# Layer 1 of seven of eight experts as Strassen products, in an fp32 mixture-of-experts kernel with two task towers

## What is computed

```python
B, D, E, T = 512, 1024, 8, 2; H1, H2, DO = 1024, 512, 256; TH1, TH2 = 512, 256
h = relu(einsum('bi,eio->beo', x, eW1) + eb1)          # layer 1: 8 experts, 1024 x 1024
h = relu(einsum('beh,eho->beo', h, eW2) + eb2)         # layer 2: 1024 x 512
expert_out = einsum('beh,eho->beo', h, eW3) + eb3      # layer 3: 512 x 256
gates = softmax(einsum('bi,tie->bte', x, gW) + gb)
tin = einsum('bte,bed->btd', gates, expert_out)
th = relu(einsum('btd,tdh->bth', tin, tW1) + tb1)
th = relu(einsum('bth,tho->bto', th, tW2) + tb2)
out = sigmoid(einsum('bth,tho->bto', th, tW3) + tb3)
```

## Time and profile before

| | us |
|---|---|
| median of 3 runs | 606.9 (606.57 to 607.07) |
| the profiled execution | 606.77 |
| its span in the profile | 605.0 |
| PE busy | 600.1 (2,629 matmuls) |
| DVE busy | 281.4 |
| ACT busy | 191.7 |
| POOL busy | 39.0 |

### The profile page before, as it was taken

One profiled execution on the slowest core, in us unless ns is written; L12 is line 12 of the kernel. 1 busy time (PEld: TensorE's weight loads), 2 busy tenths in 40 slices (PEclk: granted clock), 3 DMA queues, 4 the chain that ended last, 5 costly groups with the idle time before them and its releaser, 6 DMA issues.

```text
span 605.0 us, 7134 instructions
## 1 busy us (share of the span) xinstructions
PE 600.1 (99%) x2629; PEld 491.6 (81%) x2629; DVE 281.4 (47%) x391; ACT 191.7 (32%) x227; POOL 39.0 (6%) x37
## 2 busy tenths in 40 slices
PE   9999999999999999999999999999999999999998
PEld 5888888888888888888888888888888888888775
DVE  7634346346245343364443562453433634435592
ACT  3422325214233233223332242332332233322543
POOL 1000000030000200030000300003000300003000
PEclk9999999999999999999999999999999999999999
DMA  8930098205331073302522053310733025220000
GB/s 312 324 104 1 3 357 280 94 0 204 108 104 35 0 243 104 104 0 96 181 94 79 0 189 123 104 35 0 243 104 104 0 81 196 92 81 0 1 1 0
DMA packets 33435, 63.25 MB, mean 105 GB/s; under 512 B 1921, under 2 KB 7169, under 8 KB 33298
## 3 DMA queue, kind: packets, MB, share of 16 engines
q1 hardware_dynamic: 33106, 58.64, 29.5%
q0 software_dynamic: 176, 4.23, 1.8%
q10 hardware_dynamic: 144, 0.26, 0.1%
HBM read 63.08 MB, written 0.04 MB: 104 GB/s over the span
## 4 chain that ended last, share of the span: by engine, by line
PE 97%; DMA 1%; DVE 1%; ACT 1%; SPq 0%; issue 0%; ACTq 0%
PE bank L199 32%; PE bank L201 32%; PE bank L200 32%; DMA w_raw<-eW 1%; DVE w_lo L535 0%; ACT w_hi L440 0%; PE bank L354 0%; PE bank L353 0%; PE bank L424 0%; SPq L221 0%; DVE gated L713 0%; DVE h_lo L548 0%; ACT task_in L527 0%; ACT gated L523 0%; PE bank L371 0%
## 5 line engine op out<-in xcount | busy, mean ns | idle before, releaser
L535 DVE TENSOR_TENSOR w_lo<-w_raw,w_hi 128x1024 fp32r<-128x1024 f32 x99 | 121.0, 1224 | 239.2 <-ACT w_hi L440 238.9
L199 PE MATMUL bank<-x_hi,w_hi 128*128 128x512 f32 x524 | 204.1, 389 | 0.5 <-issue 0.4
L201 PE MATMUL bank<-x_hi,w_lo 128*128 128x512 f32 x524 | 203.9, 389 | 0.0
L200 PE MATMUL bank<-x_lo,w_hi 128*128 128x512 f32 x524 | 203.8, 389 | 0.0
L440 ACT ACTIVATE w_hi<-w_raw 128x1024 fp32r<-128x1024 f32 x99 | 104.8, 1059 | 282.7 <-PE bank L201 262.8
L199 PE MATMUL bank<-h_hi,w_hi 128*128 128x512 f32 x336 | 131.1, 390 | 0.1
L200 PE MATMUL bank<-h_lo,w_hi 128*128 128x512 f32 x336 | 130.8, 389 | 0.0
L201 PE MATMUL bank<-h_hi,w_lo 128*128 128x512 f32 x336 | 130.7, 389 | 0.0
L199 PEld LDWEIGHTS bank<-x_hi,w_hi 128*128 128x128 f32 x524 | 98.3, 188 | 21.8 <-issue 0.8
L201 PEld LDWEIGHTS bank<-x_hi,w_lo 128*128 128x128 f32 x524 | 98.4, 188 | 20.5
L200 PEld LDWEIGHTS bank<-x_lo,w_hi 128*128 128x128 f32 x524 | 98.4, 188 | 20.4
(11 more groups left out here) (61 smaller groups left out, 74.8 us busy)
## 6 DMA issues: line engine op xcount, KB each, us to landing
w_raw<-eW SPq DMA_DIRECT2D x103, 512.0 KB, 4.1
gates_all<-gates_dram POOLq DMA_DIRECT2D x1, 4096.0 KB, 14.3
w_raw<-tW SPq DMA_DIRECT2D x4, 512.0 KB, 3.4
gates_all<-xT SPq DMA_DIRECT2D x7, 256.0 KB, 6.5
w_raw<-eW SPq DMA_DIRECT2D x2, 256.0 KB, 4.3
gates_all<-xT ACTq DMA_DIRECT2D x1, 256.0 KB, 3.4
prm<-small SPq DMA_DIRECT2D x1, 164.0 KB, 8.0
gates_dram<-turned POOLq DMA_DIRECT2D x1, 32.0 KB, 2.0
```

The lines of the kernel that those rows point to most:

```text
L199: pe.matmul(bank[:], weights_hi, moving_hi, start=first, stop=False)
L200: pe.matmul(bank[:], weights_hi, moving_lo, start=False, stop=False)
L201: return pe.matmul(bank[:], weights_lo, moving_hi, start=False, stop=last)
L535: dve.tensor_tensor(w_lo[:, j % RING, :], raw_piece(j), w_hi[:, j % RING, :].bitcast(F32), ALU.subtract).then_inc(w_ready, 1)
```

## The change

Layer 1 of expert 0 stays as it was. For experts 1 to 7 the product W1ᵀx is cut into 2x2 blocks: the inner dimension into two halves of four k tiles, the output into m tiles i and i+4 (a pair, four of them), the batch into halves of 256 columns. Each pair is seven block products in place of eight (Strassen's scheme in Winograd's form, with 15 sums), each of 4 k tiles by 3 matmuls of 256 columns: 84 matmuls to a pair, 336 to an expert.

- Four sums are of x alone. They are made once, in expert 0 (`sum_x`, `t_cast`, `split_t`), into `t_hi` and `t_lo`.
- Four are of weights: DVE adds blocks of 128x512 (`sum31` makes two at once, `sum2`, `sum4`). Three weight blocks are used as they are. So each pair has 7 blocks of 128x512 to split: ACT and DVE do 3 + 2 + 2 of them (`plain`, `sums31`, `sums24`; in pair 2 the last two singly).
- Seven sums are of results. Each product has half a bank of its own. ACT takes one of them with both signs (`p1_take`), DVE makes the sums in five operations (`combine_base` and `_united` two each, `_lower` one, `_cross` two, the last three of 256 columns), and ACT and DVE split a pair's two hidden tiles (`pair_h1`, `pair_h1_lo`). DVE does the sums of pair i-1 between the weight sums of pair i+1.
- The ring has 10 slots of 128x512, the raw buffer four units of 128x1024; W1 of a pair is one transfer of 128x2048 (1 MB) from an array laid out for it on the host. W3 takes two slots of the same ring.
- Elsewhere: the high part of a hidden tile is now written by ACT straight from the bank (a second ACT operation, in place of DVE's cast), and DVE forms relu and difference in one operation; layer 2 takes its k tiles in the order 0, 4, 1, 5 ...; the gates of one expert are loaded at a time by POOL; `gated` has two buffers, so DVE's third gate product waits for POOL's first add. Layers 2 and 3 and the towers have the matmuls that they had.

```diff
+SLOT = 512
+RING = 10
+UNIT = 2 * SLOT
+UNITS = 4
...
+PAIRS = H1 // P // 2
+KK = KX // 2
...
+PRODUCTS = [(1, 0, "x", 1, 0),
+            (0, 0, "x", 0, 0),
+            (3, 0, "t", 1, 0),
+            (2, 1, "t", 0, 1),
+            (2, 0, "t", 0, 0),
+            (1, 1, "t", 1, 1),
+            (3, 1, "x", 1, 1)]
+NP = len(PRODUCTS)
...
-BANK_HIDDEN1 = [4, 5, 6, 7, 0, 1, 2, 3]
-BANK_HIDDEN2 = [6, 7, 0, 1]
-BANK_OUT3 = [4, 5]
...
+BANK_HIDDEN1 = [0, 1, 2, 3, 4, 5, 6, 7]
+BANK_HIDDEN2 = [4, 5, 6, 7]
+BANK_OUT3 = [0, 1]
...
+def used(e, u):
+    return USED0 + (e - 1) * USED + u + 1
+def free(e, u):
+    if u < NP:
+        return USED0 + (e - 1) * USED - 6 + u
+    return USED0 + (e - 1) * USED + u - RING + 1
...
+        X_SUMS = [((0, 1), (0, 0), (0, 0)),
+                  ((0, 1), (1, 1), (0, 1)),
+                  ((1, 1), (0, 0), (1, 1)),
+                  ((1, 0), (1, 1), (1, 0))]
...
+            def pair(e, i):
+                ready = splits(e) + 3 * i
+                for n, (bank, nh, source, kh, xh) in enumerate(PRODUCTS):
+                    if n == 0:
+                        if i == 0:
+                            pe.wait_ge(gated_ready, 1 + GATED * (e - 1))
+                        elif i == 1:
+                            pe.wait_ge(h2_staged, K3 * e)
+                        else:
+                            pe.wait_ge(combined, PAIRS * (e - 1) + i - 1)
+                        pe.wait_ge(slot_ready, ready + 1)
+                    if n == 3:
+                        pe.wait_ge(slot_ready, ready + 2)
+                    if n == 5:
+                        pe.wait_ge(slot_ready, ready + 3)
+                    slot = (NP * i + n) % RING
+                    to = banks[4 * (i % 2) + bank][:, nh * HALF:(nh + 1) * HALF]
+                    hi, lo = (x_hi, x_lo) if source == "x" else (t_hi, t_lo)
+                    for kk in range(KK):
+                        cols = slice(kk * P, (kk + 1) * P)
+                        mm = triple(pe, to, w_hi[:, slot, cols], w_lo[:, slot, cols],
+                                    block_of(hi, kh, xh)[:, kk, :], block_of(lo, kh, xh)[:, kk, :],
+                                    kk == 0, kk == KK - 1)
+                    mm.then_inc(slot_used, 1)
...
+            def plain_hi(e, i):
+                u = 2 * (i % 2)
+                if u == 0:
+                    act.wait_ge(landed[0], (3 + 4 * (e - 1) + i // 2 + 1) * DMA)
+                else:
+                    act.wait_ge(landed[2], (3 + 3 * (e - 1) + i // 2 + 1) * DMA)
+                pair_free(e, i, NP * i + 2)
+                act.activation(wide(pair_slots(i, 0, 3)), w_raw[:, u * UNIT:u * UNIT + 3 * SLOT], ACT.Copy) \
+                    .then_inc(slot_hi, 1)
...
+            def take_hidden2(done, m):
+                act.wait_ge(l2_done, K3 * (done - 1) + m + 1)
+                bank, bias = banks[BANK_HIDDEN2[m]], prm_of("b2", done * K3 - K3 + m)
+                if m < 2:
+                    act.wait_ge(h1_ready, K2 + PAIRS * (done - 1))
+                else:
+                    act.wait_ge(h2_ready, K3 * (done - 1) + m - 1)
+                act.activation(h2_hi[:, m, :], bank[:], ACT.Relu, bias=bias)
+                act.activation(stage[:, m % 2, :], bank[:], ACT.Identity, bias=bias).then_inc(h2_staged, 1)
...
+            def sum31(e, i):
+                landed_pair(e, i)
+                dve.wait_ge(slot_ready, splits(e) + 3 * i if i > 0 else splits(e - 1) + 3 * PAIRS)
+                dve.tensor_tensor(sums[:, 0:2, :], raw_blocks(i, 1, 2),
+                                  raw_blocks(i, 3, 1).broadcast_to([P, 2, SLOT]), ALU.add).then_inc(summed, 1)
+            def sum2(e, i):
+                dve.wait_ge(summed, 3 * PAIRS * (e - 1) + 3 * i + 1)
+                dve.tensor_tensor(sums[:, 2, :], sums[:, 1, :], raw_blocks(i, 1, 1)[:, 0, :],
+                                  ALU.add).then_inc(summed, 1)
+            def sum4(e, i):
+                dve.wait_ge(summed, 3 * PAIRS * (e - 1) + 3 * i + 2)
+                dve.tensor_tensor(sums[:, 3, :], sums[:, 2, :], raw_blocks(i, 0, 1)[:, 0, :],
+                                  ALU.add).then_inc(summed, 1)
...
+            def combine_base(e, i):
+                dve.wait_ge(p1_staged, PAIRS * (e - 1) + i + 1)
+                dve.wait_ge(slot_used, used(e, NP * i + 5))
+                if i == 0:
+                    dve.wait_ge(h2_ready, K3 * e)
+                else:
+                    dve.wait_ge(h1_ready, K2 + PAIRS * (e - 1) + i)
+                dve.tensor_tensor(quarter[:, 0:5:4, :], bank_of(i, 1), p1[:], ALU.add).then_inc(based, 1)
+            def combine_united(e, i):
+                dve.wait_ge(based, PAIRS * (e - 1) + i + 1)
+                dve.tensor_tensor(quarter[:, 1:3, :], bank_of(i, 2), quarter[:, 4:5, :].broadcast_to([P, 2, HALF]),
+                                  ALU.add).then_inc(united, 1)
+            def combine_lower(e, i):
+                dve.wait_ge(united, PAIRS * (e - 1) + i + 1)
+                dve.scalar_tensor_tensor(quarter[:, 3, :], bank_of(i, 2)[:, 0, :], prm_of("b1", e * K2 + MG + i),
+                                         quarter[:, 2, :], ALU.add, ALU.add).then_inc(lowered, 1)
+            def combine_cross(e, i):
+                dve.wait_ge(slot_used, used(e, NP * i + 6))
+                dve.scalar_tensor_tensor(quarter[:, 1, :], bank_of(i, 3)[:, 1, :], prm_of("b1", e * K2 + i),
+                                         quarter[:, 1, :], ALU.add, ALU.subtract)
+                dve.wait_ge(lowered, PAIRS * (e - 1) + i + 1)
+                dve.scalar_tensor_tensor(quarter[:, 2, :], bank_of(i, 3)[:, 0, :], prm_of("b1", e * K2 + MG + i),
+                                         quarter[:, 2, :], ALU.add, ALU.add).then_inc(combined, 1)
...
             with dve.Fori(1, E) as e:
-                expert(e)
+                sum31(e, 0)
+                sum2(e, 0)
+                sum4(e, 0)
+                plain_lo(e, 0)
+                sums31_lo(e, 0)
+                for m in range(K3 - 1):
+                    hidden2_lo(e, m)
+                sums24_lo(e, 0)
+                hidden2_lo(e, K3 - 1)
+                for i in range(PAIRS - 1):
+                    if i > 0:
+                        combine_base(e, i - 1)
+                    sum31(e, i + 1)
+                    if i > 0:
+                        combine_united(e, i - 1)
+                    sum2(e, i + 1)
+                    if i > 0:
+                        combine_lower(e, i - 1)
+                        combine_cross(e, i - 1)
+                    sum4(e, i + 1)
+                    plain_lo(e, i + 1)
+                    if i > 0:
+                        pair_h1_lo(e, i - 1)
+                    sums31_lo(e, i + 1)
+                    sums24_lo(e, i + 1)
+                combine_base(e, PAIRS - 2)
+                combine_united(e, PAIRS - 2)
+                combine_lower(e, PAIRS - 2)
+                combine_cross(e, PAIRS - 2)
+                pair_h1_lo(e, PAIRS - 2)
+                w3_lo(e)
+                for i in range(3):
+                    w2_lo(e, i)
+                combine_base(e, PAIRS - 1)
+                combine_united(e, PAIRS - 1)
+                combine_lower(e, PAIRS - 1)
+                combine_cross(e, PAIRS - 1)
+                pair_h1_lo(e, PAIRS - 1)
+                w2_lo(e, 3)
                 gate_expert(e)
...
+                        dve.wait_ge(added, GATED * (done - 1) + n + 1)
```

More of the change, by code:

```diff
@@ L197, in triple @@
         def triple(pe, bank, weights_hi, weights_lo, moving_hi, moving_lo, first, last):
[L199 to L201 removed]
+            pe.matmul(bank, weights_hi, moving_hi, start=first, stop=False)
+            pe.matmul(bank, weights_hi, moving_lo, start=False, stop=False)
+            return pe.matmul(bank, weights_lo, moving_hi, start=False, stop=last)
@@ new lines, in layer2 @@
+            def layer2(e, between=None):
+                first = isinstance(e, int)
+                order = by_tile(range(0, 6), MG) + by_bank(range(6, 8), MG)
+                for i, (n, m) in enumerate(order):
+                    k = ORDER2[n]
+                    if m == 0:
+                        if n % 2 == 0:
+                            pe.wait_ge(slot_ready, (KX + n // 2 + 1) if first
+                                       else splits(e) + 3 * PAIRS + 1 + n // 2 + 1)
+                        if first:
+                            pe.wait_ge(h1_ready, k + 1)
+                        elif n % 2 == 0:
+                            pe.wait_ge(h1_ready, K2 + PAIRS * (e - 1) + n // 2 + 1)
+                    if n == 0:
+                        if first:
+                            pe.wait_ge(h1_staged, MG + m + 1)
+                        elif m == 0:
+                            pe.wait_ge(combined, PAIRS * e)
+                    cols = slice(m * P, (m + 1) * P)
+                    mm = triple(pe, banks[BANK_HIDDEN2[m]][:], w_hi[:, n, cols], w_lo[:, n, cols],
```

(50 more changed lines are left out.)

688 lines of the change are left out of this document (395 added, 293 removed).

## The result

| | before | after |
|---|---|---|
| median of 4 runs beside each other, us | 606.74 | 586.72 |
| all runs, us | 606.38 to 607.07 | 586.29 to 587.12 |
| ratio after to before, 95% interval | | 0.967 (0.9653 to 0.9687) |
| the profiled execution and its span, us | 606.8, 605.0 | 586.58, 584.9 |

The forecast was 586. Of two of the later kernels one execution each (627.87 us at a granted clock of 0.85, and 1637.12 us) stands far from the other five and is left out of the times given here.

The account below looks back on a forecast made before the run. The prediction took PE, busy 99% of the span, to bound the kernel. 606.8 less 22.2 for layer 1, plus 0.5 at the loop's entry and 1.0 at the end, gave 586 us; range 571 to 604.

Parts of the forecast that it names:

- step 1: Layer 1, experts 1 to 7: 336 matmuls of 256 columns at 0.1201 us replace 192 of 0.2267, saving 22.2 us.
- the lead of 0.11: In layer 1, a weight load must begin 0.11 us ahead of its matmul, not its full recorded 0.188.
- Both rivals on the pace: Layer 1's 256-column matmuls take 0.1134 us, 572 in all (chance 0.17), or a whole load's 0.188, 746 (chance 0.10).
- step 2: Loop: DVE needs 10.0 us a pair against PE's 10.1, margin 3 us before layer 2, no stall in a steady expert.
- T = 0: The end of layer 2, from which the prediction counted DVE's schedule through an expert.
- DVE late: Loop: unmeasured result sums run slower, pair 3's results come 2.6 us behind layer 3, 18 us back, 604; chance 0.13.
- DVE's busy time: Whole kernel: DVE busy rises to about 465 us, ACT to about 290, costing nothing while the margins hold.
- step 3: Weight transfers in 1 MB pieces, issued 13 to 20 us ahead of their sums, and POOL's gate loads: no cost.
- step 4: Expert 0 and loop entry: added DVE work hidden in expert 0, but DVE enters the loop late, +0.5 us.
- the fast-pace rival: Layer 1: the extra 13 ns shrink with the columns, 0.1134 us a matmul, 572 us in all; chance 0.17.
- step 5: Last layers and towers: PE restarts 3.12 us behind the last bank, first gate product at 4.4; +1.0 us for both.

Follow-up runs that it names:

- the first experiment: Changed kernel plus nine series of 24 matmuls of various widths and types before the loop, into a bank nobody reads: 617.03 us.
- the second: Kernel before, with layer 1 of experts 1 to 7 issued as two halves of 256 columns, no Strassen: 624.73 us, ratio 1.0295.
- experiments 3 and 4: Changed kernel plus an unread DVE reduction in two turns of each expert: about 2.3 us an expert, 587.92 us; about 6.5 us, 612.53 us.
- Experiment 5: Changed kernel with the gates turned halfway through expert 0's layer 2 instead of three quarters through: 585.69 us, ratio 0.9653.
- experiments 3 and 8: Changed kernel plus unread work: DVE reductions, about 2.3 us an expert, 587.92 us; or POOL additions, six an expert and one before the loop, 587.78 us.
- Experiment 6: Changed kernel with the third tower piece split before the last hidden tiles, the fourth's low part behind the towers' inputs: 585.62 us, ratio 0.9652.

## Why the prediction was right, step by step

**PE's pace (step 1).** Right in value and in kind: 0.120 against 0.1201, an expert 67.54 against 67.56. That the 13.4 ns do not shrink with the columns is shown by the first experiment, and their whole price by the second. That they are a cost of each load and matmul holds for full fp32r tiles alone, and the lead of 0.11 is not shown as the cause of the floor. Both rivals on the pace fall with the same rows: 256 columns with full tiles take neither half of 227 ns nor a load's 188.

**DVE in the loop (step 2).** The schedule held to a few tenths. Counted from T = 0, here 347.52, with the forecast in brackets: pair 1 split at 9.5 (9.5), a turn 9.85 (10.0), pair 3's results done at 42.7 (42.9), the last piece of W2 at 46.2 (46.5), the gates' products at 50.3 (50.7). The row behind 42.7 is DVE's last result sum of pair 3. PE starts layer 3 at 387.83 and layer 2, whose first matmul waits for the sum, 5.4 later, so the margin is 3.1 where 3 was said:

```profile
387.83 0.40 PE L264 MATMUL bank<-h_hi,w_hi 128*128 128x512 f32 x1
...
389.73 0.47 DVE L828 SCALAR_TENSOR_TENSOR scratch<-bank,prm,scratch 128x256 f32<-128x256 f32 x1
```

The result sums on halves of a bank or with a repeated operand had no row before. They cost what was taken: 0.60 from start to start (0.66 assumed), and 0.39 for 256 columns (0.40). What the timeline has of one turn:

```profile
356.99 0.68 DVE L808 TENSOR_TENSOR scratch<-bank,scratch 128x512 f32<-128x512 f32 x1
357.59 1.22 DVE L763 TENSOR_TENSOR scratch<-w_raw 128x1024 f32<-128x1024 f32 x1
358.73 0.68 DVE L813 TENSOR_TENSOR scratch<-bank,scratch 128x512 f32<-128x512 f32 x1
...
360.32 0.48 DVE L825 SCALAR_TENSOR_TENSOR scratch<-bank,prm,scratch 128x256 f32<-128x256 f32 x1
360.71 0.48 DVE L828 SCALAR_TENSOR_TENSOR scratch<-bank,prm,scratch 128x256 f32<-128x256 f32 x1
```

The rival "DVE late" had the right kind of wait, with 3 us of slack ahead of it, and experiments 3 and 4 bound that slack in a steady expert: 2.3 us are free, 6.5 cost 2.8. Its place was wrong for the most part: 2.1 us of the stand are at the start of pair 3 and only 0.6 before layer 2, where the prediction had put all of it. The total came out all the same, because layer 2 has the least room (3.9 with what DVE gains back, against 4.4 at pair 3) and so sets the sum of both stands. The prediction had the room at the pairs as well: 4 for the same split of pair 2.

**DVE's busy time** was said to be 465 and is 436, ACT's 290 and is 264. The term was mis-sized by its bookkeeping: I had added recorded durations, and consecutive operations overlap by 0.08 in the record. The recorded durations of all operations in the new trace do add up to 465 for DVE and 285 for ACT; the page counts overlapping time once. The term entered no sum.

**Transfers (step 3).** "Each is issued 13 to 20 us ahead of its sum" was wrong for one in four: the next expert's pair 0 is issued 5 us ahead of its first sum, which then waited 0.92 us for it (the mark at 398.69 above). The other three are issued 12.5 to 23.6 us ahead. 1 MB lands in 4.8 us, under twice the 3.7 of 512 KB, as said. The late transfer cost nothing, because DVE is far ahead there.

**The entry (step 4).** 0.5 said, 0.57 measured to the start of the first matmul. But "expert 1 starts its pair 1 about 2.4 us late" was counted only in the fast-pace rival, for pair 3. It should have been read against pair 1 itself: the split that its first matmul waits for ends at 87.28, where PE would have started at 87.23.

```profile
85.53 1.75 DVE L727 TENSOR_TENSOR w_lo<-w_raw,w_hi 128x1536 fp32r<-128x1536 f32 x1
```

That is 0.2 of the missed 0.30; the other 0.1 is the slow second matmul behind the entry's own gap. Experiment 5 shows that all of it hangs on DVE's lateness. The losses of experiments 3 and 8 are in the same expert, where every delay of DVE costs PE time soonest.

**The end (step 5).** 3.1 said for the restart, 2.98 measured; 4.4 for the first gate product, 4.33 measured; +1.0 in all, 0.96 measured. Experiment 6 takes the pieces away and the time with them.

## What to carry to other kernels

Trading multiplications for additions pays on TensorE only after its tax on narrow matmuls: here 18 of 40 us went to the fixed 13.4 ns of an fp32r matmul with its load. Read that tax from starts at two widths, or measure it by itself, before the scheme is chosen, and stay above the width below which the pace no longer falls (111 ns here). When the engine that does the additions is nearly level with the bound, look for the stretch in which it enters late, the first pass of a loop above all: the steady pass can have slack that the first hasn't, and moving one early job there gave back more than the visible gap.
